# A router's scores on Trainium2: two rounded weight parts side by side in 16 columns

## The chip, the cores and the metric

The kernel runs on one core of one Trainium2 chip. The metric is device time in microseconds (us) for the whole program, one launch. Timed runs of the kernel before: 1694.19 us as the median of three (1693.38 to 1694.59).

The engines are named as in the profile: PE is TensorE's products, PEld its weight loads (of the same engine; a load can run beside a product), DVE VectorE, ACT ScalarE, POOL GpSimd, SP SyncE.

## The reference

The input x is 8 sequences of 1024 tokens of 256 numbers. Four blocks follow one another, each on a layer norm of x and each added to x: gated linear attention with a feed-forward layer, a mixture of experts, a recurrent network (tanh, 16 states), and the same mixture of experts again. The change is in the mixtures:

```python
logits = x @ router_w.T                      # 8 experts
probs = softmax(logits)
topk_vals, topk_idx = top_k(probs, 2)
topk_w = topk_vals / (topk_vals.sum(-1) + 1e-06)
expert_out = einsum('nh,eho->eno', x, expert_weights)
out = ((expert_out[topk_idx] + topk_vals) * topk_w).sum(over the two)
```

The kernel computes all eight experts for every token and weighs them with coefficients that are zero but for the two chosen ones.

## The kernel before

Time is cut into 32 rounds of 32 time steps, so a round has 256 tokens (8 sequences x 32 steps, two tiles of 128). Eight stages of the network work on eight consecutive rounds at once: in one pass of the loop body, stage 2 does attention for round n-2, stage 4 the first mixture (called m1) for round n-4, stage 5 and 6 the recurrence, stage 6 and 7 the second mixture (m2). Eight passes are written out, the middle is a loop, seven more drain it. Each engine's order is written by hand in its own `body`, and engines meet through semaphores. A wait holds up all that stands behind it on its engine.

What sets PE's order is the recurrence: 32 steps a round, each `step(k)`: a product of 8 columns (L1271), two tanh on ACT (L566, L567), a subtraction on DVE that writes `hs` (L858), and then the next step's product, which waits for that `hs`. Between two steps stands other PE work of about 1.5 us, mostly six products of a pair of experts (`moe`, through `product`, L1254).

Products in float32r take one pass; a number is split into a rounded lead and a rest, and `product` adds three of the four combinations. Plain fp32 products take two passes each (a product then counts as two in the trace).

The scores (logits) of a mixture go this way, for m1 and m2 alike:
- the normed tokens are transposed (L1260), rounded and split into `yT` (lead on ACT, rest on DVE, L953);
- `logits` (L1285): four fp32 products, one for each part and each half of the 256 features. The weights `rw` are 8 columns padded with zeros to 32 (`ROUTED = 32`), and each product has its own 32 columns of the array and its own 32 rows of the result, so the four can run side by side;
- ACT copies the 128 x 256 result out of PSUM (L696 for m1, L734 for m2);
- `logits_by_token` (L1292): two transposes bring it back, 128 columns for each tile of tokens;
- DVE adds the four pieces of each score (L898), finds the two highest (L903, L912), and the softmax and the coefficients follow on ACT and DVE.

In PE's order m1's scores stand behind step 8 and the transposes of the attention's input and of m2's input; its transposes by token stand behind the first pair of experts and ahead of step 10. m2's scores stand behind step 14, between the two halves of `attend` (L1331); its transposes stand behind step 16 and ahead of the gate product (`hTs,wz`).

Of the kernel before, what the change touches and what calls it, by code (L numbers as in the profile page):

```python
# [6 lines left out]
F32 = mybir.dt.float32  # L7
F32R = mybir.dt.float32r
U32 = mybir.dt.uint32
ALU = mybir.AluOpType  # L10
# [28 lines left out]
PAIRS = E // 2  # L39
ROUTED = 32  # L40
GROUPS = TILES * PAIRS
# [55 lines left out]
def build(nc, x, wts, out):  # L97
    ctx = ExitStack()
    with ctx:
        def sb(name, shape, dt=F32):  # L100
            return ctx.enter_context(nc.sbuf_tensor(name, shape, dt))
# [32 lines left out]
        wz = sb("wz", [P, 2, KC, P], F32R)  # L134
        rw = sb("rw", [P, KC, ROUTED])

# [90 lines left out]
        def raw(base, n):  # L227
            return stage[:, base:base + n]
# [4 lines left out]
                        (b2g[:], wts["gk_b2"])]  # L233
        late_sync = [(raw(W_1, KC * FF), wts["W1"]), (rw[:, :, 0:E], wts["router_w"]), (b1[:], wts["b1"])]
        late_sync += [(cT[:, :, n * N:(n + 1) * N], wts["C"]) for n in range(3)]
# [146 lines left out]
        def _(pool):  # L382
# [5 lines left out]
            g.memset(cw[:].bitcast(F32), 0.0)  # L388
            g.memset(rw[:], 0.0)
            g.memset(hs[0:ROW_LEAD].bitcast(F32), 0.0)  # L390
# [142 lines left out]
        def _(act):  # L533
# [13 lines left out]
            def split_late():  # L547
                act.wait_ge(sem("weights_psum"), 2)
                act.wait_ge(sem("a_loaded"), A_LOADED)
                act.wait_ge(sem("late"), LATE)  # L550
                a.activation(a_lead, a_raw, ACT.Copy)
                a.activation(cw[ROW_LEAD:ROW_LEAD + 1, :], bout[ROW_LEAD:ROW_LEAD + 1, :], ACT.Copy)
                a.activation(bout_lead, bout[ROW_REST:ROW_REST + 1, :], ACT.Copy)
                a.activation(cw_lead, ps[0:NB, BANK["RB"], 0:D], ACT.Copy).then_inc(sem("weights_lead"), 1)
                act.wait_ge(sem("weights_rest"), REST["scaled_out"])
                a.activation(wa[:, 0, W_O:W_END], raw(W_O, W_END - W_O), ACT.Copy).then_inc(sem("weights_lead"), 1)
# [63 lines left out]
            def body(it):  # L620
# [73 lines left out]
                if live(it, 5):  # L694
                    act.wait_ge(sem("LT1"), c5)
                    a.activation(m1.y[:, 0, :], ps[:, BANK["L1"], 0:TOK], ACT.Copy).then_inc(sem("lT1"), 1)  # L696
                if live(it, 7):
# [34 lines left out]
                if live(it, 7):  # L732
                    act.wait_ge(sem("LT2"), c7)
                    a.activation(m2.y[:, 0, :], ps[:, BANK["L2"], 0:TOK], ACT.Copy).then_inc(sem("lT2"), 1)  # L734
                if live(it, 6):
# [87 lines left out]
        def _(dve):  # L823
# [15 lines left out]
            def split_late():  # L839
                dve.wait_ge(sem("weights_lead"), LEAD["late"])  # L840
                v.tensor_tensor(wa[:, 1, W_O:W_END], raw(W_O, W_END - W_O), wa[:, 0, W_O:W_END].bitcast(F32), ALU.subtract).then_inc(sem("weights_rest"), 1)

# [52 lines left out]
            def top_two(m, bank, count):  # L895

                pieces = ps[:, bank, TOK:2 * TOK].rearrange("p (i s w) -> p i s w", i=TILES, w=ROUTED)[:, :, :, 0:E]
                v.tensor_reduce(m.lg, pieces.rearrange("p i s e -> p i e s"), AX.X, ALU.add).then_inc(sem(f"lg{m.s}"), 1)  # L898
                target = value(dve, count)
                dve.wait_ge(sem("pads_zero"), 1)  # L900
                dve.wait_ge(sem(f"lg{m.s}"), target)
                for i in range(TILES):
                    ins = v.max(m.mx[:, i, :], m.lg[:, i, :])  # L903
                ins.then_inc(sem(f"mx{m.s}"), 1)
# [326 lines left out]
        def _(pe):  # L1231
# [48 lines left out]
            def logits(m, bank):  # L1280

                for part in range(2):
                    for c in range(KC):
                        g = part * KC + c
                        ins = t.matmul(ps[ROUTED * g:ROUTED * (g + 1), bank, 0:TOK], rw[:, c, :], m.yT[:, part, c, :].bitcast(F32),  # L1285
                                       start=True, stop=True, skip_group_check=True)
                return ins

            def logits_by_token(m, bank):

                for i in range(TILES):
                    ins = t.transpose(ps[:, bank, TOK + i * P:TOK + (i + 1) * P], m.y[:, 0, i * P:(i + 1) * P], ident)  # L1292
                return ins
# [42 lines left out]
            def body(it):  # L1336
# [201 lines left out]
                if live(it, 4):  # L1538
                    pe.wait_ge(sem("yT1"), c4)
                    if isinstance(it, int) and it == 4:  # L1540
                        pe.wait_ge(sem("weights_rest"), REST["experts"])
                    for name, count in readers(it, "G1_0"):
                        pe.wait_ge(sem(name), count)
                    moe(m1, 0, BANK["G1_0"]).then_inc(sem("moe1"), 1)
                    pe.wait_ge(sem("lT1"), c4)
                    logits_by_token(m1, BANK["L1"]).then_inc(sem("L1"), 1)
# [47 lines left out]
                if live(it, 6):  # L1594
                    pe.wait_ge(sem("lT2"), c6)
                    logits_by_token(m2, BANK["L2"]).then_inc(sem("L2"), 1)
# [76 lines left out]
```

## Time and profile before

| | |
|---|---|
| median of 3 timed runs | 1694.19 us |
| span of the profiled execution | 1692.7 us |
| PE busy | 1591.6 us (94%) |
| PEld busy | 1324.5 us (78%) |
| DVE busy | 1274.3 us (75%) |
| ACT busy | 1051.2 us (62%) |
| POOL busy | 823.1 us (49%) |
| chain that ended last | PE 82%, DVE 6%, issue 3%, DMA 3% |

The profile gives the span of one execution, from its first instruction to its last; the timed runs lie about 1.5 us above it. PE's busy time is not time at full use: products are pipelined, and the end of each is modelled, so two that follow one another closely overlap in the record. The chain is followed back from the last instruction, at each step to what released it.

### The profile page before, as it was taken

Reading aid. Unit: us, or ns where it says so; the run is one execution under the profiler, and the core shown is the slowest. Engines: PE = TensorE matmul, PEld = TensorE weight load, DVE = VectorE, ACT = ScalarE, POOL = GpSimd, SP = SyncE. Lnnn points to the kernel's source line nnn. Section 1 sums busy time; section 2 is a strip of 40 time slices with the busy share of each in tenths; the row PEclk is TensorE's granted clock in tenths of the full one; section 3 lists DMA queues with packets and bytes.
Section 4 is the critical chain, followed back from the end, with each engine's and each line's share of the span. In section 5 each row is a group of like instructions: output and inputs, shape, how many; then the busy total and the mean of one; then the engine's idle time right before and its main releaser. Section 6 shows DMA issues by size and latency. Waiting matters only on the chain.

```text
span 1692.7 us, 51627 instructions
## 1 busy us (share of the span) xinstructions
PE 1591.6 (94%) x16840; PEld 1324.5 (78%) x16840; DVE 1274.3 (75%) x4556; ACT 1051.2 (62%) x3851; POOL 823.1 (49%) x1294
## 2 busy tenths in 40 slices
PE   4588999999999999999999999999999999998866
PEld 3477888888888888888888888888888888887654
DVE  4566777887788778787888787887888877876544
ACT  4656666666766666666666666666666667655431
POOL 3554454554555455545454554454545545543211
PEclk7799999999999999999999999999999999999978
DMA  5211111111111111011111111111111111110000
GB/s 151 84 57 45 52 58 58 42 39 43 43 56 56 56 51 43 31 52 47 56 56 56 46 42 35 50 50 56 56 56 43 37 44 44 52 52 8 7 7 13
DMA packets 117250, 81.49 MB, mean 48 GB/s; under 512 B 42016, under 2 KB 108224, under 8 KB 117056
## 3 DMA queue, kind: packets, MB, share of 16 engines
q1 hardware_dynamic: 116208, 80.10, 15.4%
q8 instruction: 38, 0.62, 0.2%
q10 hardware_dynamic: 976, 0.54, 0.1%
q14 instruction: 28, 0.23, 0.0%
HBM read 47.06 MB, written 33.55 MB: 48 GB/s over the span
## 4 chain that ended last, share of the span: by engine, by line
PE 82%; DVE 6%; issue 3%; DMA 3%; ACT 2%; SPq 2%; POOL 1%; ACTq 0%; DVEq 0%; POOLq 0%
PE ps L1254 62%; PE ps L1260 4%; PE ps L1271 4%; PE ps L1285 2%; PE ps L1301 2%; PE ps L1442 2%; PE ps L1331 2%; DMA xag<-in_x 2%; PE ps L1321 2%; PE ps L1312 1%; DVE hs L858 1%; DVE att L947 1%; DVE dstate L1075 1%; PE ps L1292 1%; DMA arow<-att 1%
## 5 line engine op out<-in xcount | busy, mean ns | idle before, releaser
L1254 PE MATMUL ps<-we,yT 128*128 128x512 f32 x3072 | 824.5, 411 | 0.3 <-DVE h2Ts L953 0.3
L1254 PEld LDWEIGHTS ps<-we,yT 128*128 128x128 f32 x3072 | 546.5, 191 | 100.9 <-issue 1.1
L566 ACT ACTIVATE h_lead<-ps 48x8 fp32r<-48x8 f32 x1024 | 172.4, 168 | 443.8 <-PE ps L1271 430.3
L858 DVE SCALAR_TENSOR_TENSOR hs<-ps,cst,h_lead 48x8 fp32r<-48x8 f32 x1024 | 224.7, 219 | 223.8 <-ACT ps L567 216.1
L1271 PEld LDWEIGHTS ps<-hs,aT 128*128 128x128 f32 x1024 | 195.1, 191 | 126.4 <-DVE hs L858 99.1
L1271 PE MATMUL ps<-hs,aT 128*128 128x8 f32 x1024 | 215.9, 211 | 39.7 <-DVE hs L858 38.3
L890 DVE SCALAR_TENSOR_TENSOR stage<-ps,coef,stage 128x256 f32<-128x256 f32 x384 | 183.1, 477 | 13.8 <-POOL stage L433 5.0
L890 DVE SCALAR_TENSOR_TENSOR acc<-ps,coef,acc 128x256 f32<-128x256 f32 x384 | 181.7, 473 | 6.6 <-POOL acc L433 2.7
L518 POOL TENSOR_TENSOR orstd<-omean,mhalf 128x32 f32<-128x32 f32 x32 | 174.6, 5455 | 0.2
L567 ACT ACTIVATE ps<-ps 48x8 f32<-48x8 f32 x1024 | 162.8, 159 | 0.0
L431 POOL TENSOR_TENSOR part<-part 128x256 f32<-128x256 f32 x64 | 46.9, 732 | 204.2 <-ACT part L584 201.8
L431 POOL TENSOR_TENSOR stage<-stage 128x256 f32<-128x256 f32 x64 | 47.8, 746 | 187.7 <-ACT stage L584 187.7
L1254 PE MATMUL ps<-h2Ts,wa 128*128 128x256 f32 x768 | 106.9, 289 | 3.7 <-DVE h2Ts L953 3.7
L1254 PE MATMUL ps<-wa,gTs 128*128 128x256 f32 x768 | 108.1, 291 | 0.7 <-DVE gTs L953 0.6
L1254 PE MATMUL ps<-wa,hTs 128*128 128x512 f32 x384 | 103.3, 406 | 0.0
L1254 PEld LDWEIGHTS ps<-wa,gTs 128*128 128x128 f32 x768 | 96.0, 191 | 7.0 <-issue 6.0
L1254 PEld LDWEIGHTS ps<-h2Ts,wa 128*128 128x128 f32 x768 | 95.8, 191 | 5.4 <-DVE h2Ts L953 3.9
L512 POOL TENSOR_SCALAR omean<-oss 128x32 f32<-128x32 f32 x32 | 8.9, 277 | 178.5 <-DVE oss L1172 178.5
L575 ACT ACTIVATE ps<-ps,lnb,lnw 128x256 f32<-128x256 f32 x128 | 67.2, 529 | 30.5 <-PE ps L1260 30.5
L1254 PEld LDWEIGHTS ps<-wa,hTs 128*128 128x128 f32 x384 | 67.6, 188 | 14.1
L401 POOL TENSOR_SCALAR ra<-mv_a 128x2 f32<-128x2 f32 x32 | 6.1, 191 | 145.0 <-DVE mv_a L877 145.0
L606 ACT ACTIVATE qx<-qt,cst 128x256 f32<-128x256 f32 x128 | 64.4, 505 | 1.4 <-DVE qt L977 1.4
(184 smaller groups left out, 3200.4 us busy)
## 6 DMA issues: line engine op xcount, KB each, us to landing
arow<-att SPq DMA_DIRECT2D x32, 512.0 KB, 2.8
atx<-arow SPq DMA_DIRECT2D x128, 128.0 KB, 2.8
vrow<-vtok SPq DMA_DIRECT2D x32, 256.0 KB, 2.1
vx<-vrow SPq DMA_DIRECT2D x128, 64.0 KB, 2.0
out<-stage SPq DMA_DIRECT2D x64, 128.0 KB
xin<-in_x SPq DMA_DIRECT2D x62, 128.0 KB
xag<-in_x SPq DMA_DIRECT2D x62, 128.0 KB
stage<-in_experts SPq DMA_DIRECT2D x1, 2048.0 KB, 9.5
```

What stands on the lines that cost most here:

```text
L431: g.tensor_tensor(m.part[:, i, 0, :], m.part[:, i, 0, :], m.part[:, i, 1, :], ALU.add).then_inc(sem(f"part{m.s}"), 1)
L518: g.tensor_tensor(orstd[:], omean[:], mhalf[:], ALU.pow).then_inc(sem("orstd"), 1)
L566: a.activation(h_lead[:], ps[0:NB, BANK["RB"], k * B:(k + 1) * B], ACT.Tanh)
L567: a.activation(h_whole, ps[0:NB, BANK["RB"], k * B:(k + 1) * B], ACT.Tanh).then_inc(sem("rnn_tanh"), 1)
L575: a.activation(ps[:, bank, c * TOK:(c + 1) * TOK], ps[:, bank, c * TOK:(c + 1) * TOK], ACT.Identity, bias=lnb[:, c:c + 1], scale=lnw[:, c: ...
L606: return a.activation(qx[:, h, :, :], bt(qt[:]), ACT.Identity, scale=headmask[:, h:h + 1])
L858: v.scalar_tensor_tensor(hs[0:NB, :, k], h_whole, keeps_rest, h_lead[:].bitcast(F32), ALU.mult, ALU.subtract).then_inc(sem("rnn_h"), 1)
L890: v.scalar_tensor_tensor(m.acc[:, i, :], ps[:, bank, half * D:(half + 1) * D], m.coef[:, i, e:e + 1], m.acc[:, i, :], ALU.mult, ALU.add).t ...
L1254: ins = t.matmul(dst, left(lp, c), right(rp, c), start=(n == 1), stop=(n == 3 * chunks))
L1260: ins = t.transpose(ps[:, dst_bank, c * TOK + i * P:c * TOK + (i + 1) * P], src[:, i, c * P:(c + 1) * P], ident)
L1271: return t.matmul(ps[0:NP, BANK["RB"], k * B:(k + 1) * B], aT[:], hs[:, :, (k - 1) % TS], start=False, stop=True, skip_group_check=True)
L1285: ins = t.matmul(ps[ROUTED * g:ROUTED * (g + 1), bank, 0:TOK], rw[:, c, :], m.yT[:, part, c, :].bitcast(F32), start=True, stop=True, skip_ ...
```

## The change

`ROUTED` becomes 16. A second weight tile `rws` holds, for each half of the features, the rounded lead of the 8 columns and beside it the rest, both float32r. `rw` loses its padding, and so the memset that zeroed it. ACT writes the leads once, DVE the rests once, at the start.

`logits` becomes four float32r products that add up in the same 16 rows of PSUM: both parts of `yT`, both halves, each against the 16 columns. They stand where the four fp32 products stood. In the built program each has a tile of 128x32 of the array, all four the same one; before it was four such tiles side by side. ACT copies 16 rows instead of 128. `logits_by_token` transposes 16 rows at a time, and writes 16 columns instead of 128 for each tile of tokens; in the built program its tile is 32x128, where it was 128x128. DVE adds two pieces of each score instead of four. Ahead of the transposes PE waits for one more semaphore, which was reached at the start of the program.

```diff
-ROUTED = 32
+ROUTED = 2 * E
...
-        rw = sb("rw", [P, KC, ROUTED])
+        rw, rws = sb("rw", [P, KC, E]), sb("rws", [P, KC, ROUTED], F32R)
...
-            g.memset(rw[:], 0.0)
...
+                a.activation(rws[:, :, 0:E], rw[:], ACT.Copy)
...
-                    a.activation(m1.y[:, 0, :], ps[:, BANK["L1"], 0:TOK], ACT.Copy).then_inc(sem("lT1"), 1)
+                    a.activation(m1.y[0:ROUTED, 0, :], ps[0:ROUTED, BANK["L1"], 0:TOK], ACT.Copy).then_inc(sem("lT1"), 1)
...
+                v.tensor_tensor(rws[:, :, E:ROUTED], rw[:], rws[:, :, 0:E].bitcast(F32), ALU.subtract)
...
-                pieces = ps[:, bank, TOK:2 * TOK].rearrange("p (i s w) -> p i s w", i=TILES, w=ROUTED)[:, :, :, 0:E]
-                v.tensor_reduce(m.lg, pieces.rearrange("p i s e -> p i e s"), AX.X, ALU.add).then_inc(sem(f"lg{m.s}"), 1)
+                pieces = ps[:, bank, TOK:TOK + TILES * ROUTED].rearrange("p (i s e) -> p i e s", i=TILES, e=E)
+                v.tensor_reduce(m.lg, pieces, AX.X, ALU.add).then_inc(sem(f"lg{m.s}"), 1)
...
+                n = 0
                 for part in range(2):
                     for c in range(KC):
-                        g = part * KC + c
-                        ins = t.matmul(ps[ROUTED * g:ROUTED * (g + 1), bank, 0:TOK], rw[:, c, :], m.yT[:, part, c, :].bitcast(F32),
-                                       start=True, stop=True, skip_group_check=True)
+                        n += 1
+                        ins = t.matmul(ps[0:ROUTED, bank, 0:TOK], rws[:, c, :], m.yT[:, part, c, :], start=(n == 1), stop=(n == 2 * KC))
...
-                    ins = t.transpose(ps[:, bank, TOK + i * P:TOK + (i + 1) * P], m.y[:, 0, i * P:(i + 1) * P], ident)
+                    ins = t.transpose(ps[:, bank, TOK + i * ROUTED:TOK + (i + 1) * ROUTED], m.y[0:ROUTED, 0, i * P:(i + 1) * P], ident[0:ROUTED, 0:ROUTED])
...
-                    pe.wait_ge(sem("lT1"), c4)
+                    target = value(pe, c4)
+                    pe.wait_ge(sem("pads_zero"), 1)
+                    pe.wait_ge(sem("lT1"), target)
```

The copy for m2 and the wait for `lT2` are changed in the same way. On PE the order stays as it was; what changes is the size of what stands there. In PE's order before, around m2's scores and transposes (`vx,atx` is `attend`, `hs,aT` a recurrence step, `we,yT` a pair of experts, `stage` m2's tokens; the first size is the output's partitions):

```order
L1331 MATMUL ps<-vx,atx 32x64 x16
L1277 REGISTER_ALU
L1271 MATMUL ps<-hs,aT 128x8
L1285 MATMUL ps<-yT,rw 32x256 x4
L1331 MATMUL ps<-vx,atx 32x64 x16
L1277 REGISTER_ALU
L1271 MATMUL ps<-hs,aT 128x8
L1254 MATMUL ps<-we,yT 128x512 x6
L1277 REGISTER_ALU
L1271 MATMUL ps<-hs,aT 128x8
L1292 MATMUL ps<-cst,stage 128x128 x2
```

The same stretch of PE in the changed program (lines are one to six further on):

```order
L1332 MATMUL ps<-vx,atx 32x64 x16
L1278 REGISTER_ALU
L1272 MATMUL ps<-hs,aT 128x8
L1287 MATMUL ps<-yT,rws 16x256 x4
L1332 MATMUL ps<-vx,atx 32x64 x16
L1278 REGISTER_ALU
L1272 MATMUL ps<-hs,aT 128x8
L1255 MATMUL ps<-we,yT 128x512 x6
L1278 REGISTER_ALU
L1272 MATMUL ps<-hs,aT 128x8
L1293 MATMUL ps<-cst,stage 128x16 x2
```

Nothing has changed places; the four score products write 16 partitions, and the two transposes 16 columns.

On DVE, at the start of the program, where the late weights are split (`att` and `dstate` belong to the first round's attention):

```order
L948 TENSOR_TENSOR att<-ps,cst 128x2x8x32 x2
L1076 TENSOR_TENSOR dstate<-ps,cst 128x512
L841 TENSOR_TENSOR rws<-rw,rws 128x2x8
L842 TENSOR_TENSOR wa<-stage,wa 128x2560
L847 TENSOR_SCALAR part<-yT,cst 48x48
```

The third row is new; the others stood there before in the same order.

## Rows read from the trace of the kernel before

**Rows 1.** The page: span, busy time, the chain that ended last.
```profile
span 1692.7 us, 51627 instructions
PE 1591.6 (94%) x16840; PEld 1324.5 (78%) x16840; DVE 1274.3 (75%) x4556; ACT 1051.2 (62%) x3851; POOL 823.1 (49%) x1294
PE 82%; DVE 6%; issue 3%; DMA 3%; ACT 2%; SPq 2%; POOL 1%; ACTq 0%; DVEq 0%; POOLq 0%
```
**Rows 2.** The chain of waits, one round: start us, us, what.
```profile
914.85 0.27 PE ps L1271
...
959.26 0.80 PE ps L1321 x46
...
960.08 0.05 DVE att L947
```
**Rows 3.** One round: its length, busy us of PE, PEld, DVE, ACT, POOL; clock.
```profile
914.80:963.40 48.60, 48.40 (x526) 40.59 (x526) 39.23 (x143) 32.35 (x121) 25.49 (x41) 1.00 0.16 48
```
**Rows 4.** Lines L1271 and L1292: ns min/median/max, first and last start.
```profile
L1271 PE MATMUL ps<-hs,aT x1024: 167/173/377, 124.4 to 1661.3; 128*128 128x8 f32 x171
...
L1292 PEld LDWEIGHTS ps<-cst,ym x64: 137/140/225, 100.0 to 1594.1; 128*128 128x128 f32 x64
L1292 PE MATMUL ps<-cst,ym x64: 269/272/416, 100.3 to 1594.3; 128*128 128x128 f32 x64
```
**Rows 5.** PE's products at m2's scores: start us, us, what, count.
```profile
924.69 0.64 PE L1285 MATMUL ps<-yT,rw 128*32 128x256 f32 x8
925.15 0.63 PE L1331 MATMUL ps<-vx,atx 128*32 128x64 f32 x32
```
**Rows 6.** PE's weight loads at m2's scores and transposes.
```profile
924.49 0.18 PEld L1271 LDWEIGHTS ps<-hs,aT 128*128 128x128 f32 x1
924.69 0.16 PEld L1285 LDWEIGHTS ps<-yT,rw 128*32 128x32 f32 x8
...
925.71 0.19 PEld L1271 LDWEIGHTS ps<-hs,aT 128*128 128x128 f32 x1
925.82 1.23 PEld L1254 LDWEIGHTS ps<-we,yT 128*128 128x128 f32 x6
...
927.32 0.20 PEld L1292 LDWEIGHTS ps<-cst,stage 128*128 128x128 f32 x2
927.49 0.78 PEld L1254 LDWEIGHTS ps<-hTs,wz 128*128 128x128 f32 x6
```
**Rows 7.** From 32x32 products back to the full array.
```profile
909.59 0.85 PE L1312 MATMUL ps<-smid,qt 32*32 32x64 f32 x64
...
910.37 0.19 PEld L1271 LDWEIGHTS ps<-hs,aT 128*128 128x128 f32 x1
```
**Rows 8.** From m1's transposes on, PE, PEld and DVE, with idle time and releaser.
```profile
918.32 0.38 PE L1292 MATMUL ps<-cst,ym 128*128 128x128 f32 x2
918.43 0.19 PEld L1271 LDWEIGHTS ps<-hs,aT 128*128 128x128 f32 x1
...
918.57 1.64 PE L1254 MATMUL ps<-we,yT 128*128 128x512 f32 x6
...
918.80 0.68 DVE L953 TENSOR_TENSOR hTs<-ps,hTs 128x512 fp32r<-128x512 f32 x1
...
919.40 0.20 DVE L898 TENSOR_REDUCE lm<-ps 128x16 f32<-128x64 f32 x1
...
920.12 0.19 PEld L1271 LDWEIGHTS ps<-hs,aT 128*128 128x128 f32 x1 [0.35 <-DVE hs L858]
...
920.26 1.65 PE L1254 MATMUL ps<-we,yT 128*128 128x512 f32 x6
...
921.70 0.19 PEld L1271 LDWEIGHTS ps<-hs,aT 128*128 128x128 f32 x1 [0.23 <-DVE hs L858]
```
**Rows 9.** Float32r loads behind one another; fp32 passes of 256 columns.
```profile
906.62 1.48 PEld L1254 LDWEIGHTS ps<-wa,gTs 128*128 128x128 f32 x12 [0.20 <-issue]
...
903.45 1.03 PE L1442 MATMUL ps<-stage,bin_ 128*128 128x256 f32 x4
```

More of the change, by code:

```diff
@@ L233, in build @@
                         (b2g[:], wts["gk_b2"])]
-        late_sync = [(raw(W_1, KC * FF), wts["W1"]), (rw[:, :, 0:E], wts["router_w"]), (b1[:], wts["b1"])]
+        late_sync = [(raw(W_1, KC * FF), wts["W1"]), (rw[:], wts["router_w"]), (b1[:], wts["b1"])]
         late_sync += [(cT[:, :, n * N:(n + 1) * N], wts["C"]) for n in range(3)]
@@ L733, in body @@
                     act.wait_ge(sem("LT2"), c7)
-                    a.activation(m2.y[:, 0, :], ps[:, BANK["L2"], 0:TOK], ACT.Copy).then_inc(sem("lT2"), 1)
+                    a.activation(m2.y[0:ROUTED, 0, :], ps[0:ROUTED, BANK["L2"], 0:TOK], ACT.Copy).then_inc(sem("lT2"), 1)
                 if live(it, 6):
@@ L1594, in body @@
                 if live(it, 6):
-                    pe.wait_ge(sem("lT2"), c6)
+                    target = value(pe, c6)
+                    pe.wait_ge(sem("pads_zero"), 1)
+                    pe.wait_ge(sem("lT2"), target)
                     logits_by_token(m2, BANK["L2"]).then_inc(sem("L2"), 1)
```

## The prediction

> **What bounds the kernel now.** I read the page first. TensorE (PE) is busy 94% of the span and the chain that ended last runs over PE for 82% of it [rows 1]. Neither number says that every PE nanosecond counts, so the chain of waits over one steady round (48.6 us) comes next. It is on PE without a break from 914.85 us, through both places that the change touches, to the state products at 959.26; only then does it pass to VectorE (DVE) at 960.08 [rows 2]. The same stretch by engine: PE busy 48.40 of 48.60 us, all others at most 40.6, clock granted in full [rows 3]. So what a round gains or loses on PE is gained or lost in the span, 32 times, unless PE stands waiting just behind it. That happens mostly behind the first of the two places, and it decides what that place costs.
>
> The busy time hides where the array is not fed, so I need four intervals. (a) A product's end in the trace lies about 0.17 us behind its last column: an 8-column product takes 0.167 at the least [rows 4]. (b) After one full 128x128 weight load the next follows 0.11 us later (925.71 to 925.82) [rows 6], and a product that had to wait for its own load gets its first column when those 0.11 are over. (c) **A change of the array's tiling.** Between full products the next load may start while the last product is being fed. From the full recurrence product at 924.49 to the first 128x32 load it takes 0.20 us, not 0.11 [rows 6]: 0.09 are lost on the way in. On the way out, the 32x32 products that start at 909.59 last 0.85; less the tail of 0.17 their last column goes in at 910.27, and the next full load starts at 910.37 [rows 7]. So 0.10 us of emptying, and then the load of 0.11 lies bare: 0.20 us to the first column. (d) Transposes: two loads take 0.20 together [rows 6], one 0.14 [rows 4], so a second one follows 0.06 behind the first; two products take 0.38 [rows 8] and one 0.27 [rows 4], so 0.11 is fed per 128 columns.
>
> **Part by part.** *The four score products.* Before, they are four column tiles with 8 passes in all, begun at 924.69; the next products start at 925.15 [rows 5]: 0.46 us. In the new program they are float32r products of 16 weight columns, all in the same tile, so they follow one another in one pass each. Float32r products of 256 columns follow at (1.48-0.19)/11 = 0.117 us (twelve loads, less the length of the last) [rows 9]. Ahead of the first column lies a short load, as before: 0.46 less two fp32 passes, 0.03 at most. With 0.02, 4 x 0.117 make 0.49: 0.03 slower than four tiles side by side. Below, the bound is 256 columns at the granted 2.4 GHz, 0.107 each and 0.45 in all (a gain of 0.01); above, two fp32 passes per product in one tile at (1.03-0.17)/4 = 0.215 [rows 9], 8 x 0.215 = 1.72 (a loss of 1.26). I take 0.03, nearest to the float32r row. For m2 it counts. For m1 it does not: the recurrence product behind it waits for hs.
>
> *The two transposes by token.* They write 16 columns instead of 128 and read 16 partitions instead of 128. In the new program their tile is 32x128, where the neighbours' is 128x128. That turns a place without a change of tiling into one with two changes. m2, before: fed from 927.32 (end of the 8-column product), next load 927.49, first column of the gate product 0.11 later, at 927.60 [rows 6]: 0.28 us. After: 0.09 emptying, load 0.06, second load 0.06, 16 columns 0.01, 0.09 emptying, full load 0.11 = 0.42. Loss 0.14. m1, before: first transpose fed at 918.32, load of the recurrence product at 918.43, its column at 918.54 [rows 8]: 0.22. After, from 918.32 on, again 0.42. Loss 0.20. The bounds: if this tiling needs no emptying, only the columns shrink and the loss becomes a gain of 0.05 at each place; if both changes cost as the way out does, add 0.02. No row shows a 32x128 tile beside a full one in steady state, only 128x32 and 32x32 tiles; both of them behave as in (c), so I take the loss.
>
> The Trainium skill, TensorEngine Tiling (Array Packing), section Tiling Modes, lists 32x128 as a configuration of its own and says that changing the mode, not just the tile, drains TensorE. By that rule the loss stands; the trace agrees for 128x32 and 32x32 [rows 6, 7], and no row shows it for 32x128.
>
> *What hides m1's loss.* Behind m1's transposes come six products fed from 918.57, lasting 1.64, so the last column goes in at 920.04; the recurrence product that follows waits for hs, loads only at 920.12 and is fed at 920.23 [rows 8]. Slack about 0.17. hs is late there because DVE works through a 0.68 us subtraction, the score sum (919.40) and the maxima before it; the sum is the first that needs the transposes, which end at 918.70. One step on, the same is seen smaller: six products from 920.26, 1.65 long, end feeding at 921.74; load at 921.70, fed at 921.80 [rows 8], about 0.05. Together 0.22 against 0.20: m1 costs nothing. If this cover were gone it would cost 0.20 x 32 = 6.4 us. Behind m2's place the chain stays on PE [rows 2], and each later wait hangs on a PE step that moves with it.
>
> *The rest.* The score sum on DVE reads 32 elements instead of 64; it takes 0.20 now [rows 8], of which at most half can go. It lies in m1's cover, where it brings hs nearer, and is worth at most 0.03 a round there while PE is early, nothing once PE is late. ScalarE's copies keep 256 elements per partition, no change. The added wait on a semaphore that has long been reached delays PE's queue, but the load behind it is issued under 1.4 us of running products: nothing, and a few hundredths per place if that cover failed. One small copy on ScalarE and one small subtraction on DVE come in once, before the large weight subtraction; DVE is on the path there, so 0.1 to 0.2 us once. One memset less on GpSimd lies under the first loads.
>
> **Sum.** m2: 0.14 + 0.03 = 0.17 a round; m1: 0 with 0.20 lost in 0.22 of slack; 32 x 0.17 = 5.4 us, and 0.1 at the start: 5.5. The execution profiled spans 1692.7 us [rows 1]; the median of the runs lies 1.5 above it, which I keep. 1692.7 + 5.5 + 1.5 = 1699.7 us.
>
> **Rivals.**
> 1. *No emptying for the 16-row transposes* (not slower). A tile of rows 0 to 31 over all columns may be loaded ahead like a full one. For it: every product still uses all column groups. Against it: (c) holds for both narrow tilings seen. It decides at m2: from a loss under 0.11 us a round on, the time is within the measurement. m2: -0.05 + 0.03; m1: PE is early, so only DVE's 0.03 counts: -0.05 x 32 = -1.6: 1692.6 us.
> 2. *Faster.* As 1, and the products besides keep the whole array, so that their entry goes without emptying, and run at full feed: m2 -0.05 - 0.09 - 0.01, m1 -0.03 : -0.18 x 32 = -5.8: 1688.4. Against it: the way out to the 128x32 products behind m2's scores then costs its 0.09 as well, which takes the gain to -2.9 (1691.3).
> 3. *m1's cover fails*: hs moves with PE instead of standing still, because DVE's score sum comes to wait for the transposes. Against it: they end 0.7 us before it starts [rows 8]. 5.5 + 6.4: 1706.1.
> 4. *Float32r in a narrow tile falls back to fp32 passes*: m2 1.26 + 0.14, m1 1.26 + 0.20 - 0.22: 2.64 x 32 = 84: 1779. Against it: nothing in the trace, for it shows no such product; for it nothing either.
>
> The Trainium skill, PSUM — Partial Sum Buffer, in The four PSUM rules, says that float32r matmuls force all column groups. By that rule the products would stay whole-array, the entry without emptying and the exit with it, and the forecast would move by two hundredths a round; no run so far shows it.
>
> **How the numbers follow.** Forecast 0.52, with its own range 1696.5 to 1702.5 (transposes' loss 0.10 to 0.18, products -0.01 to 0.05, m1's remainder up to 0.05); rival 1 0.22; rival 2 0.09; rival 3 0.13; rival 4 0.04. The range for 8 in 10 takes in rival 1 and rival 3 and leaves out rival 4 and most of rival 2: 1691 to 1707. What can be told from no change here is 0.2%, 3.4 us, so from 1690.8 to 1697.6. Slower: 0.52 less a tenth of it at its lower edge, and rivals 3 and 4: 0.64. Within: rival 1, that tenth, and a third of rival 2: 0.29. Faster: 0.07.
>
> **What would show it.** In the changed profile: the transposes' loads no longer start while the product before them is fed, but about 0.09 later, and the time from the recurrence product to the gate product at m2 grows from 0.28 to about 0.42. The score products stand one behind another, 0.11 to 0.12 apart, and their block takes about 0.49. A round takes 48.8 us instead of 48.6. PE's wait for hs behind m1 (0.35 on the load) shrinks to under 0.1. The prediction is wrong if the transposes' loads stay ahead, if the score products are over 0.2 apart, or if the round grows by more than 0.3.

## The result, and the profile after

The changed kernel takes 1702.26 us (median of 14 runs, 1693.74 to 1708.13), the kernel before, run beside it, 1695.07 us (14 runs, 1690.40 to 1700.72). The ratio is 1.0029, with a 95% interval of 1.0017 to 1.0042: 4.9 us slower, where 5.5 were forecast. The two medians by themselves lie 7.2 us apart (1.0042), the upper end of that interval; compared at the same clock (below) the kernels are 4.6 us apart. The profiled execution spans 1697.7 us against 1692.7 [rows 1].

The page after, its span, busy times and chain, answering to [rows 1]:

```profile
span 1697.7 us, 51180 instructions
PE 1596.6 (94%) x16584; PEld 1329.7 (78%) x16584; DVE 1271.4 (75%) x4557; ACT 1053.3 (62%) x3852; POOL 821.9 (48%) x1293
PE 83%; DVE 6%; issue 3%; DMA 2%; ACT 2%; POOL 1%; SPq 1%; ACTq 0%; DVEq 0%; POOLq 0%
```

The trace counts 256 products fewer (four passes instead of eight in each of the 64 blocks of scores), and yet PE is busy 5.0 us longer, by as much as the span grew. A product's record runs on about 0.17 us past its last column, (a) in the prediction, and so covers the time in which the array is being emptied: the busy time can't show this loss.

To find the place I measured, in each trace, the time from the end of one recurrence product to the end of the next. There are 32 such steps in a round; the median over rounds 4 to 23 leaves out the start, the end and single late transfers (us, worked out from the rows of the recurrence product):

```
step                          before   after    change
round                         48.616   48.827   +0.211
9-10   m1's transposes         1.727    1.931   +0.204
10-11  behind it               1.681    1.510   -0.171
11-12  behind that             1.578    1.523   -0.055
14-15  m2's score products     1.219    1.275   +0.056
16-17  m2's transposes         0.994    1.139   +0.145
each of the other 27 steps                      within 0.015
```

m1's loss is given back in the two steps behind it; m2's two places add 0.201, and the other 27 steps together 0.03. The mean of those 20 rounds grew by less, 0.173 us: in the trace of before four of them have an m2 step that is 0.04 to 0.40 longer, behind a late transfer of x (see the last experiment), in the trace after only one, by 0.03.

m2 in the trace after, PE and weight loads (start us, us, what), answering to [rows 5, 6]:

```profile
927.48 0.19 PEld L1272 LDWEIGHTS ps<-hs,aT 128*128 128x128 f32 x1
...
927.59 0.36 PEld L1287 LDWEIGHTS ps<-yT,rws 128*16 128x16 f32 x4
927.62 0.63 PE L1287 MATMUL ps<-yT,rws 128*16 128x256 f32 x4
...
928.17 0.49 PEld L1332 LDWEIGHTS ps<-vx,atx 128*32 128x32 f32 x32 [0.23 <-issue]
...
928.76 0.19 PEld L1272 LDWEIGHTS ps<-hs,aT 128*128 128x128 f32 x1
...
930.36 0.17 PE L1272 MATMUL ps<-hs,aT 128*128 128x8 f32 x1
930.46 0.20 PEld L1293 LDWEIGHTS ps<-cst,stage 16*128 16x128 f32 x2
...
930.68 0.77 PEld L1255 LDWEIGHTS ps<-hTs,wz 128*128 128x128 f32 x6
```

Before, the recurrence product ahead of m2's transposes started together with their first load, which is in [rows 6]:

```profile
927.32 0.17 PE L1271 MATMUL ps<-hs,aT 128*128 128x8 f32 x1
```

At the transposes the prediction's reading holds: the first load starts 0.10 behind the product, the gate product's load starts at 930.68 and is done 0.11 later: 0.43 us from product to product, forecast 0.42, before 0.28. At the score products it doesn't hold: the first load comes 0.11 behind the recurrence product's load, where it was 0.20. No emptying on the way in. It is on the way out: the load of the 128x32 products waits (0.23 of idle loads).

m1, with DVE, answering to [rows 8]:

```profile
921.43 0.29 PE L1293 MATMUL ps<-cst,ym 16*128 16x16 f32 x2
...
921.65 0.19 PEld L1272 LDWEIGHTS ps<-hs,aT 128*128 128x128 f32 x1
...
921.76 1.23 PEld L1255 LDWEIGHTS ps<-we,yT 128*128 128x128 f32 x6
...
921.82 0.68 DVE L954 TENSOR_TENSOR hTs<-ps,hTs 128x512 fp32r<-128x512 f32 x1
...
922.42 0.17 DVE L899 TENSOR_REDUCE lm<-ps 128x16 f32<-128x32 f32 x1
...
922.85 0.20 DVE L859 SCALAR_TENSOR_TENSOR hs<-ps,cst,h_lead 48x8 fp32r<-48x8 f32 x1
...
923.11 0.19 PEld L1272 LDWEIGHTS ps<-hs,aT 128*128 128x128 f32 x1
...
923.27 0.17 PE L1272 MATMUL ps<-hs,aT 128*128 128x8 f32 x1
...
924.69 0.19 PEld L1272 LDWEIGHTS ps<-hs,aT 128*128 128x128 f32 x1 [0.19 <-DVE hs L859]
```

hs is written at 923.05 (922.85 + 0.20, DVE), and the first load behind m1 now starts at 923.11, 0.12 behind the end of the loads before it (922.99), where it was 0.35; the prediction had said under 0.1. The load stands ready before the product is fed (923.27): here PE became the bound. The next load still waits, 0.19 where it was 0.23. Over 320 to 1300 us the loads' wait for hs fell as the slack was used up (total us, times, longest; first the kernel before, then after):

```profile
PEld ps L1271 <- DVE hs L858: 39.0, 121, 0.5
```
```profile
PEld ps L1272 <- DVE hs L859: 26.9, 100, 0.5
```

**The scatter of the runs.** Single runs of one kernel differ by up to 14 us, three times the effect. They go with the mean granted clock of the run: of the changed kernel, a run at 0.977 spanned 1691.7 us and one at 0.966 spanned 1705.2. A least-squares fit over the 181 runs of all kernels below except the one in fp32 (one level per kernel, one common slope) gives 1.13 us per 0.001 of clock and leaves 1.7 us of scatter. The kernel before ran on three chips beside the experiments, and at the same clock its mean is 1697.3, 1697.4 and 1697.3 us there, so the levels can be compared across them; the 14 runs of before beside the result have no clock on record and aren't in the fit. The steady stretch is not where the scatter comes from: between 320 and 1300 us every profiled execution ran at 1.00, the upper of the two levels, as in [rows 3]. The clock is lower at the start and behind 1300 us, where PE has gaps. Of the changed kernel, first PE's busy share and its granted clock, in tenths, over 40 slices of 42 us: in the first four slices the clock is 0.7 to 0.9 and PE busy by 0.4 to 0.8. Then the windows (window; its length; busy us of PE, PEld, DVE, ACT, POOL; clock): behind 1300 us it is 0.96, with PE busy 333 of 360 us.

```profile
PE   4588999999999999999999999999999999998866
PEclk8798999999999999999999999999999999999978
```
```profile
917.91:966.74 48.83, 48.59 (x519) 40.72 (x519) 39.23 (x143) 32.46 (x121) 25.50 (x41) 1.00 0.16 48
...
1220.00:1300.00 80.00, 79.77 (x788) 67.51 (x779) 64.16 (x227) 54.68 (x200) 40.54 (x60) 1.00 0.12 38
1300.00:1660.00 360.00, 332.80 (x3010) 274.45 (x2978) 253.50 (x971) 203.21 (x820) 148.77 (x238) 0.96 0.11 34
```

The table has each kernel's timed ratio, its level at the same clock (0.972, from the fit, with about 95%), and its steady round:

```
kernel           ratio to before (95%)     us at clock 0.972   round us
before           1                         1697.3 +- 0.4       48.616
after            1.0029 (1.0017, 1.0042)   1701.9 +- 0.9       48.827
rows72, twice    0.9983 (0.9968, 0.9998)   1696.3 +- 0.7       48.617
                 0.9995 (0.9978, 1.0012)                       48.632
products_only    1.0015 (0.9999, 1.0030)   1696.7 +- 1.0       48.666
narrow_m1        0.9995 (0.9978, 1.0011)   1697.6 +- 1.1       48.649
narrow_m2        1.0016 (0.9998, 1.0033)   1699.8 +- 1.1       48.805
rows64           1.0048 (1.0030, 1.0067)   1703.3 +- 1.1       48.889
twice_m1         1.0036 (1.0015, 1.0057)   1705.3 +- 1.1       48.915
mixed            1.0010 (0.9995, 1.0025)   1701.1 +- 1.0       48.837
waits_only       one run, 1698.10                              48.633
wide_products    one run, 1698.34                              48.676
fp32_products    one run, 1765.29                              50.818
```

### The profile page after: what moved, and what is told of

The parts are those of the page before. It is cut to its first block, busy times and chain, and to the rows that moved or that the text cites. A ratio compares the mean times of both kernels' runs of the same rounds, so it can differ in the third digit from the quotient of the medians.

```text
span 1697.7 us, 51180 instructions
## 1 busy us (share of the span) xinstructions
PE 1596.6 (94%) x16584; PEld 1329.7 (78%) x16584; DVE 1271.4 (75%) x4557; ACT 1053.3 (62%) x3852; POOL 821.9 (48%) x1293
## 4 chain that ended last, share of the span: by engine, by line
PE 83%; DVE 6%; issue 3%; DMA 2%; ACT 2%; POOL 1%; SPq 1%; ACTq 0%; DVEq 0%; POOLq 0%
PE ps L1255 63%; PE ps L1261 4%; PE ps L1272 4%; PE ps L1287 2%; PE ps L1332 2%; PE ps L1302 2%; PE ps L1443 2%; PE ps L1322 2%; PE ps L1313 1%; DVE hs L859 1%; DMA xag<-in_x 1%; DVE att L948 1%; DVE dstate L1076 1%; PE ps L1293 1%; POOL orstd L517 1%
## 5 line engine op out<-in xcount | busy, mean ns | idle before, releaser
L1272 PE MATMUL ps<-hs,aT 128*128 128x8 f32 x1024 | 210.8, 206 | 39.2 <-DVE hs L859 38.7
```

Of the source, the lines that this page charges most:

```text
L1272: return t.matmul(ps[0:NP, BANK["RB"], k * B:(k + 1) * B], aT[:], hs[:, :, (k - 1) % TS], start=False, stop=True, skip_group_check=True)
```

## The experiments

The theory: the transposes of 16 rows stand in a narrow row tile, so the array's tiling changes ahead of them and behind them, and each time the array is emptied first (the next load starts about 0.1 us later). At m1 slack hides it, at m2 nothing does. The rivals: the score products cost the time, the added wait does, or m1's cover fails.

### The same transposes in the full tile

In the changed kernel, both pairs take 72 rows and columns instead of 16 (rows 16 to 71 hold stale numbers; DVE's sum reads the same 16 columns for each tile of tokens, now 128 apart). In the built program their tile is 128x128, as before the change:

```
-  t.transpose(ps[:, bank, TOK + i*ROUTED:TOK + (i+1)*ROUTED], m.y[0:ROUTED, 0, ...], ident[0:ROUTED, 0:ROUTED])
+  rows = 72 if m.s == 1 else 72
+  t.transpose(ps[:, bank, TOK + i*P:TOK + i*P + rows], m.y[0:rows, 0, ...], ident[0:rows, 0:rows])
```

> The changed kernel, but both pairs of transposes take 72 rows and write 72 columns instead of 16 (rows 16 to 71 hold stale numbers that nothing reads). The score products are those of the changed kernel. Theory (the narrow row tile of the transposes is what costs: array emptied on the way in and out): with more than 64 rows the transposes lie in the same 128x128 tile as their neighbours, so both losses go: step with m1's transposes back from 1.93 to 1.73 us, step with m2's from 1.139 to about 0.99 or, since 56 columns less are fed per transpose, 0.95; m2's score products stay at +0.056 a round. A round of 48.62 to 48.66 us, 1694 to 1696 by the median against 1695 before: no difference from before, 5 us less than the changed kernel. Rival (the score products cost the time, by what they leave behind them): nothing comes back, a round of 48.83, 1.003 of before. Rival (it is the wait on the second semaphore ahead of the transposes): the same, 48.83.

Measured: m1's step 1.683 us, m2's 0.958, m2's scores 1.266 (+0.047), round 48.617. The loss at both transposes is gone, and both steps are shorter than before by 0.045 and 0.036, the 112 columns that are no longer fed. m2's transposes here (PE and loads): the load starts with the recurrence product again, and 0.96 us lie between the two recurrence products.

```profile
927.63 0.17 PE L1272 MATMUL ps<-hs,aT 128*128 128x8 f32 x1
927.64 0.20 PEld L1294 LDWEIGHTS ps<-cst,stage 72*128 72x128 f32 x2
...
928.59 0.17 PE L1272 MATMUL ps<-hs,aT 128*128 128x8 f32 x1
```

Neither the score products nor the wait can be the main cost, since both are still there. The kernel is 5.6 us faster than the changed one at the same clock. Against the kernel before, it was timed a second time:

> The 72-row kernel once more, word for word, beside the mixed one: its steady round equals that of before to 0.01 us, yet its timed ratio was 0.9983, 0.9968 to 0.9998. Theory (that ratio was chance at the edge of its interval): a ratio between 0.9985 and 1.001. Rival (a real gain outside the steady rounds): 0.997 to 0.9985 again.

The second ratio was 0.9995. The two together stand at -1.0 us, 0.06%: at the edge of what the fit tells apart, and not the 0.17% of the first ratio alone. The steady rounds (48.617, 48.632, against 48.616 before) say no gain.

### Eight rows decide

The same kernel with 64 rows and columns instead of 72; in the built program the tile is now 64x128:

```
-  rows = 72 if m.s == 1 else 72
+  rows = 64 if m.s == 1 else 64
```

> The 72-row kernel with 64 rows and 64 columns per transpose. Theory (the tile decides, not the number of rows): 64 rows lie in a 64x128 tile, so with 8 rows fewer both changes of tiling are back: m2's step from 0.958 up to 1.139 plus what 96 more columns take than in the changed kernel (0.04 at the full clock), 1.14 to 1.18 us; m1's step 1.683 to 1.93 to 1.97, of which 0.22 is given back in the two steps behind it. The round 48.80 to 48.86 us, 1.003 to 1.004 of before. Rival (the loss grows with the rows left idle, or only a 32-row tile empties): m2's step stays at 0.95 to 1.0 and the round at 48.62.

```profile
934.42 0.17 PE L1272 MATMUL ps<-hs,aT 128*128 128x8 f32 x1
934.52 0.20 PEld L1294 LDWEIGHTS ps<-cst,stage 64*128 64x128 f32 x2
...
935.60 0.17 PE L1272 MATMUL ps<-hs,aT 128*128 128x8 f32 x1
```

Eight rows fewer, and the load again starts 0.10 behind the product; m2's step is 1.186 us against 0.958. m1's step is 1.973, of which 0.24 come back behind it. Round 48.889, a little above the expected 48.86, and 7.0 us more than with 72 rows. So it is the tile that costs, not the number of idle rows. This kernel is slower than the changed one by its 96 more columns, without any gain from them.

The Trainium skill, TensorEngine Tiling (Array Packing), section Tiling Modes, lists 64x128 beside 32x128 as modes of their own, and 128 rows as "No Row Tiling"; that changing the mode drains the engine is borne out by this run for 64x128 and by the changed kernel for 32x128 (the load 0.10 behind the product in each).

### One place at a time

From the 72-row kernel, m1's pair alone, and m2's pair alone, go back to 16 rows:

```
narrow_m1:  rows = 16 if m.s == 1 else 72
narrow_m2:  rows = 72 if m.s == 1 else 16
```

> As the kernel with 72 rows, but m1's transposes alone are back at 16 rows. Theory (m1's loss of 0.20 us a round lies in PE's wait for hs): the step with m1's transposes 1.73 to 1.93, the two steps behind it shorter by 0.17 and 0.03 to 0.05, the round and the time those of the 72-row kernel within 0.02 us a round (0.5 us). Rival 3 of the prediction (hs moves with PE and the cover fails): a round longer by 0.20 us, 6 us in all, 1.0035.

> As the kernel with 72 rows, but m2's transposes alone are back at 16 rows. Theory: m2's step 0.95 to 0.99 becomes 1.139 us, nothing behind it gives that back, a round of 48.80 to 48.84 us and the time of the changed kernel within 1 us (5 to 6 us over the 72-row kernel). Rival (the cost is at m1): the time of the 72-row kernel.

Measured for m1 alone: its step 1.933 us, the two behind it 1.510 and 1.515, the round 48.649, 0.03 above the 72-row kernel: a hundredth over the expected 0.02. By the fit it is 1.3 us above it (+-1.3). Rival 3, 6 us, is out.

For m2 alone: its step is 1.140, nothing is given back, and the round is 48.805. The fit has 3.5 us above the 72-row kernel and 2.1 (+-1.4) below the changed one, where I expected 5 to 6 and under 1: by time this expectation was missed, by the round it was met.

About 1 us of that lies outside the steady rounds, where m1's pair is not covered. The three steps from the one with m1's transposes on, together, in us:

```
m1's rows                steady   round 1   28      29      30
72 (rows72)              4.960    4.701     4.703   4.703   4.701
16 (narrow_m1)           4.951    4.957     4.955   4.956   4.936
72 (narrow_m2)           4.963    4.694     4.703   4.697   4.701
16 (after)               4.965    4.935     4.936   4.948   4.956
```

In these four rounds the step behind m1 takes 1.51 us with either form, the length that it has in a steady round once the wait for hs is gone. There is no slack to give the loss back, and m1's 16 rows cost 0.25 us a round, 1.0 in all. That is most of the 1.3 us by which narrow_m1 stands above the 72-row kernel and half of the 2.1; the rest of the 2.1 is within its error.

The products without the narrow transposes:

```
+  rows = 128 if m.s == 1 else 128
```

> The changed kernel with the old transposes, 128 rows and 128 columns each; what is left of the change is the four float32r score products in 16 rows, the copies of 16 rows, the score sum over 32 elements and the added waits. Theory: only m2's step with the score products is longer, 1.219 to 1.275 us; the score sum's 0.03 us less on VectorE helps m1's step a little or not: a round of 48.62 to 48.67, 1.000 to 1.001 of before. If the products cost what the blind sum gave (0.03 a round), 0.5 to 1 us are all of it. Rival (score products are the cost): 1.003.

m2's score step is 1.275 again (+0.056), the transposes' steps are those of before (1.730, 0.992), round 48.666. The ratio of 1.0015 looked like more, but its runs had the lowest clock of all (0.9705): at the same clock it is 0.6 us below before. m1's next step is 0.038 shorter, as far as the shorter score sum goes (DVE's sum takes 0.17 instead of 0.20).

### How much cover m1 has left

```
+  logits_by_token(m1, BANK["L1"])
   logits_by_token(m1, BANK["L1"]).then_inc(sem("L1"), 1)
```

> The changed kernel with m1's two narrow transposes issued twice in a row (four products in the same tile, same result). Theory (m1's loss is covered only up to the 0.22 us of slack, and 0.20 of it is used): the second pair needs no change of tiling, so it adds two loads and two times 16 columns, 0.12 to 0.14 us, to the step with m1's transposes (1.93 to 2.05 or 2.07), and almost nothing of it is given back behind: a round 0.10 to 0.14 longer than the changed kernel's 48.83, 3 to 4.5 us, 1.005 of before. Rival (there is still cover): the steps behind shorten by as much, and the round stays at 48.83. If each transpose empties the array by itself, the step grows by 0.3 or more.

Measured: m1's step 2.055 us (+0.124 over the changed kernel), the steps behind it 1.504 and 1.511 (-0.006, -0.012), round 48.915, +0.088 on the median, a little under the 0.10 to 0.14 expected; at the same clock +3.4 us (expected 3 to 4.5). Four loads in one tile take 0.32 where two take 0.20, so a further transpose adds 0.06 and no emptying. The load behind them no longer waits for hs:

```profile
928.33 0.32 PEld L1293 LDWEIGHTS ps<-cst,ym 16*128 16x128 f32 x4 [0.37 <-issue]
...
928.68 0.19 PEld L1272 LDWEIGHTS ps<-hs,aT 128*128 128x128 f32 x1
...
930.05 0.19 PEld L1272 LDWEIGHTS ps<-hs,aT 128*128 128x128 f32 x1
...
931.58 0.19 PEld L1272 LDWEIGHTS ps<-hs,aT 128*128 128x128 f32 x1
```

The two steps behind m1 have now given back 0.177 and 0.067 against before. With 64 rows it was 0.171 and 0.072, of a loss of 0.245. So the cover is about 0.24 us in all and is used up: m1 was free only because its loss was the size of the slack. The same change with four transposes would have lost on both places.

### The wait alone

The kernel before, with the extra wait at both places:

```
-  pe.wait_ge(sem("lT1"), c4)
+  target = value(pe, c4)
+  pe.wait_ge(sem("pads_zero"), 1)
+  pe.wait_ge(sem("lT1"), target)
```

> The kernel before with nothing changed but a register value and a wait on a long reached semaphore ahead of each pair of transposes, as the changed kernel has them. Theory: PE's queue has 1.4 us of running products to hide them under, all steps as before within 0.01 us, round 48.60 to 48.63. Rival (the wait costs): the steps with the transposes grow by 0.03 to 0.2.

All steps at the two places are as before (1.728, 1.219, 0.994); round 48.633, in one run. The wait costs nothing, as costed.

### In which tile the score products stand

Two edits of the 72-row kernel. In its built program the float32r products of 16 columns are given a tile of 128x32, as was said with the change. First the weights are padded by zeros to 128 columns, with which the built program has 128x128:

```
-  rws = sb("rws", [P, KC, ROUTED], F32R)   ... t.matmul(ps[0:ROUTED, bank, 0:TOK], rws[:, c, :], ...)
+  rws = sb("rws", [P, KC, P], F32R)        ... t.matmul(ps[:, bank, 0:TOK], rws[:, c, :], ...)
```

> The 72-row kernel with the router's 16 columns padded by zeros to 128, so that each score product has a 128x128 tile by its shape. Theory (float32r products of 16 columns already stand in the whole array, and the change of tiling at m2 lies behind them, ahead of the 128x32 products): only the load is longer, by no more than the 0.11 of a full one against 0.09; the first score load stays 0.11 behind the recurrence product's load, the products 0.117 apart, and the load of the next 128x32 product stays about 0.09 behind their feed. m2's step 1.266 to 1.29 us, round 48.62 to 48.66. Rival (the products stood in the same narrow tile as the 128x32 products behind them, as the blind sum has it): the place of the emptying moves from ahead of the products to behind them, and m2's step changes by more than 0.03.

```profile
926.25 0.19 PEld L1273 LDWEIGHTS ps<-hs,aT 128*128 128x128 f32 x1
926.36 0.53 PEld L1288 LDWEIGHTS ps<-yT,rws 128*128 128x128 f32 x4
927.02 0.49 PEld L1334 LDWEIGHTS ps<-vx,atx 128*32 128x32 f32 x32
```

A size was missed: the step is 1.355 us, not 1.27 to 1.29. By its size alone, 0.09 more, this would have been the rival's sign; what speaks against the rival is where the loads stand. The place of the loads is as expected: 0.11 behind the recurrence product's, as with 16 columns (924.75, 924.86 in the 72-row kernel), and in both the 128x32 loads start 0.10 behind the last column of the scores. The 0.09 come from the first load, which nothing hides: 128 columns take 0.11 before the first column can be fed, 16 columns, by the difference, about 0.02; behind the first product the others follow 0.117 apart in both. I had counted the load's length in its row (94 ns against 188) as if both were exposed alike. The round, 48.676, is 0.06 above that of the 72-row kernel, less than the 0.09 of this step, because other steps are up to two hundredths shorter, for which I have no reason.

The Trainium skill, TensorE: Matmul & The Clock Gate, section Step-by-step: what each phase is for, says that a weight load's time goes with its columns and not with its rows. The traces agree: 188 ns at 128 columns and 94 at 16; with 16 rows instead of 128 it stays at 136 against 140.

Then the same 16 columns, read as fp32:

```
-  t.matmul(..., rws[:, c, :], m.yT[:, part, c, :], ...)
+  t.matmul(..., rws[:, c, :].bitcast(F32), m.yT[:, part, c, :].bitcast(F32), ...)
```

> The 72-row kernel with the same four 16-column score products, but read as fp32 instead of float32r. Theory (float32r alone kept them in the whole array): as fp32 they stand in a narrow column tile: the first score load comes 0.20 instead of 0.11 behind the recurrence product's load, and the loads of the 128x32 products behind them no longer wait an emptying's 0.09 more. The products take two passes, 0.215 each, 8 x 0.215 = 1.72 us, 1.25 more than now, so m2's step goes from 1.266 to about 2.5, and the round from 48.62 by 2.3 to 2.6 to 51.0 to 51.2, 1775 us. Rival (the dtype has no part in the tiling): the first score load stays at 0.11. Rival (fp32 with 256 columns takes four passes' time): m2's step above 4 us.

```profile
958.59 0.19 PEld L1272 LDWEIGHTS ps<-hs,aT 128*128 128x128 f32 x1
...
958.80 1.41 PEld L1287 LDWEIGHTS ps<-yT,rws 128*16 128x16 f32 x8
958.80 1.69 PE L1287 MATMUL ps<-yT,rws 128*16 128x256 f32 x7
960.11 0.87 PEld L1333 LDWEIGHTS ps<-vx,atx 128*32 128x32 f32 x32
...
960.32 0.38 PE L1287 MATMUL ps<-yT,rws 128*16 128x256 f32 x1
...
961.07 0.19 PEld L1272 LDWEIGHTS ps<-hs,aT 128*128 128x128 f32 x1
```

With the same shape the first load now comes 0.21 behind, and the loads of the 128x32 products start at 960.11, while the last of the eight passes (0.215 apart) is still to be fed: the emptying has moved from behind the products to ahead of them. m2's step is 2.481 as expected. The round is 50.818 and not 51.0 to 51.2: at m1 1.22 were added and 0.25 came back, the whole of m1's cover, more than I had allowed. So the array takes a 16-column product in float32r as one that fills it, whatever tile the built program names, and the same product in fp32 as a narrow one: this is what failed in the prediction's sum for the scores.

The Trainium skill, PSUM — Partial Sum Buffer, section The four PSUM rules, says that float32r matmuls force all column groups; the two traces agree (first load 0.11 behind as float32r, 0.21 as fp32).

### The cheaper form at each place

m1 as in the 72-row kernel; m2 with the four column-tiled fp32 products of the kernel before (with its padded `rw` and its copy of 128 rows) and transposes of 104 rows:

```
+  if m.s == 2:
+      for part in range(2):
+          for c in range(KC):
+              g = part * KC + c
+              ins = t.matmul(ps[32*g:32*(g+1), bank, 0:TOK], rw[:, c, :], m.yT[:, part, c, :].bitcast(F32), start=True, stop=True, skip_group_check=True)
+      return ins
-  rows = 72 if m.s == 1 else 72
+  rows = 72 if m.s == 1 else 104
```

> Each place with the form that was cheaper in the runs so far: m1 with the four float32r products in 16 rows and transposes of 72 rows, m2 with the four column-tiled fp32 products of the kernel before and transposes of 104 rows. Theory, from the steps measured: m1 -0.045 + 0.018, m2's score step back to 1.219, m2's transposes -0.036 x 24/56 = -0.015: a round of 48.57 to 48.60 us, 0.04 under before and the 72-row kernel, 1.3 us in all, which is under what the timed runs tell apart (0.9985 to 1.0000). Rival (only the profile's chance made the steps differ): 48.62. Rival (the ratio 0.9983 of the 72-row kernel is real and has a cause outside the steady rounds): the same ratio here.

It was to be the best and isn't: round 48.837, 1701.1 us at the same clock. The two steps came out as worked out where nothing else was late: scores 1.219, transposes 0.97 to 0.98 in 8 of the 20 rounds. In the other twelve that step was 1.04 to 1.94, and these are the twelve rounds in which DVE waited for a transfer of x at that place. In the one at 979 us DVE's xhat started late for want of a transfer of x, and hs, and then PE, with it:

```profile
978.55 0.41 DVE L883 TENSOR_SCALAR xhat<-xag,nrm 128x256 f32<-128x256 f32 x1 [0.23 <-DMA xag<-in_x]
...
979.87 0.21 DVE L860 SCALAR_TENSOR_TENSOR hs<-ps,cst,h_lead 48x8 fp32r<-48x8 f32 x1
...
980.14 0.27 PE L1275 MATMUL ps<-hs,aT 128*128 128x8 f32 x1
```

DVE's wait for that transfer between 320 and 1300 us (total us, times, longest), of before and of this kernel:

```profile
DVE xhat L881 <- DMA xag<-in_x: 1.2, 4, 0.5
```
```profile
DVE xhat L883 <- DMA xag<-in_x: 4.8, 12, 1.1
```

Its total was 0 to 4.6 us in the other kernels, in at most 7 rounds, so it varies by itself and the median round mostly escapes it; with twelve of 20 it doesn't. On top of it ten other steps were 0.010 to 0.013 us longer each, and one 0.040 shorter. Why the transfers came late and why those steps moved the runs don't show. The case is open, and it isn't settled whether the form of the products has a part in it.

## Why the prediction came out right, and where its steps did not

- **m2's transposes**: forecast +0.14 a round by two emptyings, a bare load and fewer columns; measured +0.145. rows72 and rows64 show that the tile does it. Right, by the stated mechanism, but not 32 times: in the last four rounds this step is 0.88 to 0.95 us before and after, because no gate product follows the transposes there and the wait for hs hides them (in round 28 the load of the next recurrence product stands idle for 0.57 us before, for 0.48 after).
- **m1's transposes**: forecast +0.20, hidden in 0.17 + 0.05. Measured +0.204, given back 0.171 and 0.055; twice_m1 and narrow_m1 show the edge of the cover. Right for the steady rounds. The sum took the cover as there in all 32; in rounds 1, 28, 29 and 30 it isn't, and the first three lost 0.18 to 0.22 each (round 30 of before can't be compared: the granted clock is 0.52 from 1591.0 to 1594.4 us, mostly the lower level, and six products of a pair of experts last 2.91 us instead of 1.64). In rounds 28 and 29 the new score products gave as much back, a gain that the sum doesn't have either: the step that holds them fell from 1.81 to 1.62 us (once 1.70) in every kernel with 16 float32r columns at m1, while in a steady round it stays at 1.86.
- **m2's score products**: forecast +0.03, measured +0.056 (+0.047 in rows72), a little above the -0.01 to 0.05 that the range was made with. The step that failed is the one that put them "all in the same tile", narrow like that of the 128x32 products behind them, with the entry's emptying kept; the built program names that tile, but they stand in the whole array. The entry costs 0.14 instead of 0.20 from the recurrence load to the first product; the block takes 0.55 (927.62 to 928.17), forecast 0.49, since the exit's emptying is in it; together 0.03 more than before, by chance the sum's own figure. The further 0.03 is a term the sum lacks: the first load of the 128x32 products was hidden, and is bare behind a change of tiling (0.59 from 928.17 to the recurrence product's load at 928.76, against 0.56 from 925.15 to 925.71 [rows 5, 6]). fp32_products bears this out: there the 128x32 loads are ahead again, and from the last column of the scores (960.32 + 0.38 - 0.17) to the recurrence load (961.07) it takes 0.54 us, before 0.55, in the changed kernel 0.68. Rival 2 had the whole array right and its balance wrong: it named the 0.09 on the way out, but not the bare load behind it.
- **The wait, and the small copies**: nothing, as forecast (waits_only). The score sum's 0.03 at m1 was hidden once PE was the bound. The 0.1 at the start wasn't measured by itself: the recurrence's first product ended 0.6 us later, 125.4 against 124.8, but between 124.2 and 126.7 in the other kernels.
- **The sum**: 32 x 0.17 = 5.4. m2 cost 0.20 in a steady round, not 0.17, the median round grew by 0.211, and 32 of those would be 6.8 us; at the same clock the kernel is 4.6 us slower (+-1.0). Of the difference 0.6 are the four rounds in which m2's transposes cost nothing; where the rest lies isn't shown. That the total came so near is partly luck: a term that was too small and a count that was too large pulled opposite ways. The forecast of 1699.7 us lies 2.6 below the median of this series; 0.9 of that is the run-to-run level of before (1695.07 against 1694.19), the rest is within the scatter of the clock. The median is 0.24 below the top of the stated range, 1702.5; the range's own terms (0.09 to 0.28 a round) would have given 1697.2 to 1703.3 and not 1696.5 to 1702.5.
- **The rivals**: 1 and 2 fell because the row tile does empty the array; 3 by narrow_m1; 4 because float32r runs in single passes, 0.117 apart.

## What to carry to other kernels

A product with fewer rows isn't cheaper when the lower row count puts it in another tile than its neighbours: with 72 rows the 112 columns saved gave 0.04 us a place, with 16 rows 224 were saved and the place still lost 0.15 to 0.20. With more than 64 rows (72 and 104 were run), even of stale data that nobody reads, the saving is kept without the loss. When a loss is covered by a wait behind it, write down how much of the cover it uses: here it was 0.20 of 0.24, and most of the next 0.12 had to be paid. And ask in which rounds the cover is there: at the start and the end of this program it wasn't.

## What the runs showed of the hardware that I had not expected

- The change of tiling lies between 64 and 72 rows: 1.186 us against 0.958 for the same step.
- A 16-column float32r product is preloaded like a full one (0.11 behind a full load) and the array is emptied behind it, ahead of a 128x32 tile; the same operands as fp32 have it the other way round (0.21 ahead, nothing behind).
- A load of few columns is nearly free where it lies bare: 0.11 us for 128 columns, 0.09 less for 16.
- Runs of one kernel differ by 1.13 us for each 0.001 of mean granted clock; comparing at the same clock turned a ratio of 1.0015 (products_only) into no loss, and gave the kernel before the same level on three chips within 0.2 us.
